# Opening stage of a cross-attention and local-attention kernel: loading, turning, normalising and projecting tokens by groups of four batches

## The reference, cut to what matters

```
z  = (x - mean(x)) / sqrt(var(x) + 1e-5)           # layer norm without scale
Q  = z @ Wq + bq ;  K = ctx @ Wk + bk ;  V = ctx @ Wv + bv
for each batch and head:                           # the "attention steps"
    p = softmax(Q_h @ K_h.T / sqrt(8)) ;  o_h = p @ V_h
x  = x + concat(o_h) @ Wo + bo
# bv is folded into the output: bo + bv @ Wo
```

## Time and profile before

| | |
|---|---|
| median of 3 runs | 2327.3 us (2323.77 to 2329.75) |
| the profiled execution | 2321.82 us, span of the profile 2320.0 us |
| busy: PE, DVE, ACT, POOL | 2133.4, 1756.9, 1709.5, 1339.4 us |
| granted clock of TensorE, mean | 0.981 |

### The profile page before, as it was taken

The page is one execution under the profiler, slowest core; times in us unless marked ns, Lnnn a source line. Parts: engine busy times, 40 slices in busy tenths (PEclk is TensorE's granted clock), DMA queues, the critical chain, the costliest instruction groups (busy, mean ns, idle before and its releaser), DMA issues. The chain is left out here.

```text
span 2320.0 us, 88291 instructions
## 1 busy us (share of the span) xinstructions
PE 2133.4 (92%) x33770; PEld 1456.9 (63%) x33770; DVE 1756.9 (76%) x4926; ACT 1709.5 (74%) x5910; POOL 1339.4 (58%) x1270
## 2 busy tenths in 40 slices
PE   6989999999999999999999999999999877899997
PEld 4656766666666666666666666666666664666663
DVE  3888877778777778777878777878777487888863
ACT  3767878877778787877888677877787544787872
POOL 1337757666666666666666566666666125666650
PEclk8999999999999999999999999999999998999998
DMA  4001221112211212112211122211121100000000
GB/s 110 4 3 34 72 55 47 39 48 66 54 41 43 62 49 55 43 44 62 57 47 41 39 67 57 49 35 47 50 55 41 44 15 6 13 17 11 15 11 23
DMA packets 141519, 96.93 MB, mean 42 GB/s; under 512 B 61832, under 2 KB 133040, under 8 KB 141104
## 3 DMA queue, kind: packets, MB, share of 16 engines
q1 hardware_dynamic: 141104, 91.28, 15.6%
HBM read 23.11 MB, written 1.05 MB: 10 GB/s over the span
## 5 line engine op out<-in xcount | busy, mean ns | idle before, releaser
L715 PE MATMUL bank<-wqkv,hs 128*128 128x512 f32 x1344 | 671.2, 618 | 20.3 <-ACT arena L1438 13.8
L1712 POOL TENSOR_TENSOR arena<-arena,rnorm 128x512 f32<-128x512 f32 x448 | 455.1, 1044 | 385.9 <-DVE rnorm L1963 384.6
L1705 POOL TENSOR_TENSOR arena<-arena 128x512 f32<-128x512 f32 x448 | 567.3, 1273 | 138.3 <-DVE arena L1912 138.1
L1407 ACT ACTIVATE arena<-bank,amx 128x64 f32<-128x64 f32 x1536 | 457.6, 334 | 7.5 <-DVE amx L1978 7.2
L1907 DVE TENSOR_TENSOR arena<-bank,rot 128x512 f32<-128x512 f32 x448 | 306.4, 684 | 88.3 <-PE bank L715 85.2
L1384 ACT ACTIVATE arena<-bank 128x512 f32<-128x512 f32 x448 | 264.1, 616 | 133.8 <-PE bank L736 132.6
L715 PEld LDWEIGHTS bank<-wqkv,hs 128*128 128x128 f32 x1344 | 229.9, 192 | 202.5 <-issue 153.6
L1407 ACT ACTIVATION_READ_ACCUMULATOR arena<-bank,amx 128x1 f32 x1536 | 351.1, 229 | 0.0
L1912 DVE TENSOR_TENSOR arena<-bank,rot 128x256 f32<-128x256 f32 x896 | 332.9, 412 | 0.0
L736 PEld LDWEIGHTS bank<-ident,arena 128*128 128x128 f32 x1792 | 213.3, 143 | 152.2 <-issue 129.1
L1919 DVE TENSOR_REDUCE ss<-arena 128x8 f32<-128x512 f32 x448 | 283.2, 669 | 32.3 <-ACT arena L1378 32.1
(11 more groups left out here) (179 smaller groups left out, 3218.0 us busy)
## 6 DMA issues: line engine op xcount, KB each, us to landing
arena<-arena SPq DMA_DIRECT2D x768, 64.0 KB
wqkv<-in_L_ffn_Wqkv_dram SPq DMA_DIRECT2D x24, 256.0 KB, 3.2
hs<-z SPq DMA_DIRECT2D x128, 32.0 KB, 1.8
fx<-z SPq DMA_DIRECT2D x32, 128.0 KB, 2.2
hs<-z SPq DMA_DIRECT2D x128, 31.8 KB, 1.9
fx<-z SPq DMA_DIRECT2D x32, 127.0 KB, 2.5
wqkv<-in_L_ffn_Wqkv_dram SPq DMA_DIRECT2D x24, 128.0 KB, 2.6
w<-in_L_ffn_W_dram SPq DMA_DIRECT2D x6, 341.0 KB
```

The lines of the kernel that those rows point to most:

```text
L715: nc.tensor.matmul(bank[o][:], src[:], wqkv[w][:, off:off + 512], start=True, stop=True).then_inc(AT[name] if part < 2 else AT[name][i], 1)
L1407: ins = nc.scalar.activation(pb[i][0][p % 2][:, h * DH:(h + 1) * DH], bank[3 + g][:, j * DH:(j + 1) * DH], ACT.Exp, bias=amx[p % 2][:, i, ...
L1705: nc.gpsimd.tensor_tensor(t, t, rs[i][c], ALU.add).then_inc(AT["ak" if c else "aq"][i], 1)
L1712: nc.gpsimd.tensor_tensor(t, t, rnorm[p % 2][:, i, HU * c:HU * c + HU].unsqueeze(2).to_broadcast([P, HU, DH]), ALU.mult).then_inc(AT["mk" ...
```

## The change

- `x` and the context land in four pieces each, by groups of four batches, with a semaphore for each group; the identity is the first load, and the other constants are spread behind the pieces. They land in tiles of their own (`raw_x`, `raw_c`), so `cen` and `dev` are no longer landing places.
- The eight loads of cross-attention weights and biases are issued by ACT on its own DMA queue.
- PE, ACT and DVE get a new order for the opening stage: the work is interleaved by group. The reciprocal square root runs once for group 0 (`pe_var(0, 1)`) and once for groups 1 to 3 (`pe_var(1, 4)`), so its 11 DVE instructions run twice. Attention steps 0 and 1 stand inside this order; group 3 is projected after step 1.
- The bfloat16 identity and the masks are made on ACT between attention steps 1 and 2.
- POOL waits for the keys and values of the group that it needs, not for all.
- Later users of the shared semaphores get other counts; nothing is changed behind attention step 16 but a wait of PE for the masks.

Core of the diff (the functions `tokens`, `context`, `x_keys` and so on are the old operations on one group):

```diff
-            sp.dma_start(cen.rearrange("p (b d) -> p b d", b=NB), A["x"].rearrange("b t d -> t b d")).then_inc(ld_x, 16)
-            sp.dma_start(dev.rearrange("p (b d) -> p b d", b=NB), A["ctx_1024"].rearrange("b t d -> t b d")).then_inc(ld_x, 16)
+            def load_tokens(k):
+                for dst, name in ((raw_x, "x"), (raw_c, "ctx_1024")):
+                    sp.dma_start(quads(group(dst, k)), A[name][4 * k:4 * k + 4].rearrange("b t d -> t b d")).then_inc(ld_x[k], 16)
+            sp.dma_start(ident[:], c_ident).then_inc(ld_x[0], 16)
+            load_tokens(0)
+            load_tokens(1)
+            sp.dma_start(head_m[:], c_head).then_inc(ld_c, 16)
+            load_tokens(2)
+            load_tokens(3)
+            sp.dma_start(v_mask[:], c_vmask.rearrange("p (h d) -> p h d", h=4)).then_inc(ld_c, 16)
...
         @block.tensor
+            turn_tokens(0)
+            turn_tokens(1)
+            pe.wait_ge(c_pool, 1)
+            first_mean(0, 4)
+            pe.wait_ge(ld_xw, 8 * 16)
+            x_keys(0, 5)
+            x_values_in(0, 6)
+            first_mean(1, 7)
+            pe_var(pe, 0, 1, 4)
+            turn_tokens(2)
+            pe.wait_ge(XP["dve"], K_READY[0])
+            x_keys(1, 5)
+            pe.wait_ge(XP["act"], V_READY[0])
+            x_values_in(1, 6)
+            turn_tokens(3)
+            first_broadcast(0, 4)
+            first_mean(2, 0)
+            first_mean(3, 2)
+            pe.wait_ge(in_act, 3)
+            x_queries(0, 1)
+            pe_var(pe, 1, 4, 7)
+            x_step(0)
+            pe.wait_ge(LN["xn"], 1)
+            first_broadcast(1, 4)
+            pe.wait_ge(XP["dve"], K_READY[1])
+            first_broadcast(2, 5)
+            pe.wait_ge(XP["act"], V_READY[1])
+            first_broadcast(3, 6)
+            x_queries(1, 7)
+            pe.wait_ge(LN["xn"], 2)
+            x_keys(2, 4)
+            pe.wait_ge(LN["xn"], 3)
+            x_values_in(2, 5)
+            pe.wait_ge(LN["xn"], 4)
+            x_queries(2, 6)
+            pe.wait_ge(XP["dve"], K_READY[2])
+            pe.wait_ge(XP["act"], V_READY[2])
+            x_step(1)
+            pe.wait_ge(XP["act"], Q_READY[1])
+            x_keys(3, 7)
+            pe.wait_ge(XP["act"], Q_READY[2])
+            x_values_in(3, 6)
+            pe.wait_ge(XP["dve"], K_READY[3])
+            x_queries(3, 7)
+            pe.wait_ge(XP["act"], Q_READY[3])
+            nc.tensor.matmul(bank[7][:, 256:257], xwo[:], xbv[:], start=True, stop=True).then_inc(X0["y"], 1)
+            for s in range(2, NB + 1):
+                x_step(s)
...
         @block.scalar
+            for i, n in enumerate(("Wq", "Wk", "Wv")):
+                act.dma_start(xw[:, i, :], A["L0_xattn_" + n]).then_inc(ld_xw, 16)
+            for i, n in enumerate(("bq", "bk", "bo")):
+                act.dma_start(xb[:, i:i + 1], col(A["L0_xattn_" + n])).then_inc(ld_xw, 16)
+            act.dma_start(xbv[:], col(A["L0_xattn_bv"])).then_inc(ld_xw, 16)
+            act.dma_start(xwo[:], A["L0_xattn_Wo"]).then_inc(ld_xw, 16)
...
+            context(0)
+            act_square(act, 0, 0)
+            x_values_in(0, 2, 6)
+            context(1)
+            act_square(act, 0, 1)
+            context(2)
+            x_values_in(1, 4, 6)
+            context(3)
+            x_queries(0, 5, 1)
+            act_square(act, 0, 2)
+            act_square(act, 0, 3)
+            x_step(0)
+            x_queries(1, 6, 7)
+            x_values_in(2, 8, 5)
+            x_queries(2, 9, 6)
+            x_step(1)
+            x_values_in(3, 11, 6)
+            x_queries(3, 12, 7)
+            masks()
+            for s in range(2, NB + 2):
+                x_step(s)
...
         @block.gpsimd
-            pool.wait_ge(XP["qe"], NBLK)
-            pool.wait_ge(XP["ve"], NBLK)
-            pool.wait_ge(XP["ke"], NBLK)
+                    pool.wait_ge(XP["act"], V_READY[b // 4])
+                    pool.wait_ge(XP["dve"], K_READY[s // 4])
...
         @block.vector
+            tokens(0)
+            tokens(1)
+            dve_centre(dve, 0, 0, 4, base_x)
+            dve.wait_ge(ld_xw, 8 * 16)
+            nc.vector.tensor_scalar(xbq[:], xb[:, 0:1], float(1 / np.sqrt(XD)), None, ALU.mult).then_inc(XP["dve"], 1)
+            x_keys(0, 1, 5)
+            dve_centre(dve, 0, 1, 7, base_x)
+            first_newton(0, 1, 4)
+            tokens(2)
+            x_keys(1, 3, 5)
+            tokens(3)
+            dve_normalise(dve, 0, 0, 4, z)
+            dve_centre(dve, 0, 2, 0, base_x)
+            dve_centre(dve, 0, 3, 2, base_x)
+            first_newton(1, 4, 7)
+            x_step(0)
+            for k in range(1, NBLK):
+                dve_normalise(dve, 0, k, 3 + k, z)
+            x_keys(2, 7, 4)
+            x_step(1)
+            x_keys(3, 10, 7)
```

More of the change, by code:

```diff
@@ L112, in build @@
         arena = sb("arena", [P, 49 * BLK])
-        cen = arena[:, 8 * TOK:9 * TOK]
-        dev = arena[:, 9 * TOK:10 * TOK]
+        raw_x, raw_c, cen, dev = (arena[:, i * TOK:(i + 1) * TOK] for i in range(4))
         slot = lambda i: arena[:, i * BLK:(i + 1) * BLK]
@@ L237, in pe_mean, with pe_var @@
                              ).then_inc(LN["mean"], 1)
[L239 to L244, removed]
+        def pe_var(pe, first, last, o):
+            pe.wait_ge(LN["sq"], last)
+            for b in range(4 * first, 4 * last):
+                c = 2 * (b - 4 * first)
+                mm = nc.tensor.matmul(bank[o][:, c:c + 2], dev[:, b * P:(b + 1) * P], mean_w[:, 0:2], start=True, stop=True)
+            mm.then_inc(LN["var"], 1)
         def pe_broadcast(k, o):
@@ L590, in _, with turn_tokens @@
         def _(pe):
-            pe.wait_ge(ld_x, 32)
-            pe.wait_ge(ld_c, 96)
-            for src, o in ((cen, 0), (dev, 4)):
-                for k in range(NBLK):
+            def turn_tokens(k):
+                pe.wait_ge(ld_x[k], 48 if k == 0 else 32)
+                for src, o in ((raw_x, 0), (raw_c, 1)):
+                    o += 2 * (k % 2)
+                    if k >= 2:
+                        pe.wait_ge(in_act if o % 2 else io_dve, k - 1)
                     for j in range(4):
@@ new lines, in _, with context @@
+            for i, n in enumerate(("Wq", "Wk", "Wv")):
[4 more added lines that the diff above has]
+            act.dma_start(xwo[:], A["L0_xattn_Wo"]).then_inc(ld_xw, 16)
+            def context(k):
+                act.wait_ge(io_ps, 2 * k + 2)
+                nc.scalar.activation(group(ctx_t, k), bank[1 + 2 * (k % 2)][:], ACT.Copy).then_inc(in_act, 1)
@@ new lines, in x_values_in, with x_queries, masks @@
+            def x_values_in(k, n, o):
+                act.wait_ge(XP["p"], n)
+                nc.scalar.activation(group(x_v, k), bank[o][:], ACT.Copy).then_inc(XP["act"], 1)
+            def x_queries(k, n, o):
+                act.wait_ge(XP["p"], n)
+                act.wait_ge(XP["dve"], BQ_READY)
+                nc.scalar.activation(group(x_q, k), bank[o][:], ACT.Identity, bias=xbq[:, 0:1], scale=float(1 / np.sqrt(XD))
+                                     ).then_inc(XP["act"], 1)
+            def masks():
+                act.wait_ge(ld_c, 80)
+                nc.scalar.activation(ident_b[:], ident[:], ACT.Copy).then_inc(XP["act"], 1)
+                for n in range(2):
+                    for a in range(2):
+                        w = DH if n == 0 else P
+                        o = 2 * DH * n + w * a
+                        nc.scalar.activation(mask_b[n][:, a], mask_f[:, o:o + w].unsqueeze(1).to_broadcast([P, 4, w]), ACT.Copy
+                                             ).then_inc(XP["act"], 1)
@@ L2256, in y_gate @@
                 ins.then_inc(YP["gt"], 1)
-            for s in range(NB + 1):
+            tokens(0)
[19 more added lines that the diff above has]
+            x_keys(3, 10, 7)
+            dve.wait_ge(X0["y"], 1)
+            nc.vector.tensor_tensor(xbo[:], bank[7][:, 256:257], xb[:, 2:3], ALU.add).then_inc(XP["dve"], 1)
+            for s in range(2, NB + 1):
                 x_step(s)
```

140 lines of the change are left out of this document (42 added, 98 removed).

## The result

| | us |
|---|---|
| before, median of 5 runs | 2324.69 (2322.69 to 2329.75) |
| after, median of 5 runs | 2311.74 (2302.56 to 2317.28) |
| ratio after / before | 0.9937, 95% interval 0.9915 to 0.9958 |
| profiled execution of after, its span | 2317.28, 2315.5 |

The change gains 13 us by the medians, 14.6 by the ratio (0.63% of 2324.7); I had said 9.6. The opening is almost what was forecast: the scores of batch 3 start at 58.40 us instead of 66.92. The surplus lies behind them, where I had expected nothing.

A forecast was written before the change was run, and what follows sets the result against it. PE was taken as the bound, with gains possible only in the first 66.92 us. Load and regrouping 12.6 us less low clock 3.0 gave 9.6 us, so 2327.3 would become 2317.7 us, range 2311 to 2324.

The forecast's parts named there:

- the low clock: PE in the opening: one fall to 1.2 GHz between 24 and 31 us, costing 3.0 us (2.5 to 6).
- whatever it moves there shifts all that follows by the same amount: Behind the first 66.92 us: only semaphore counts change, so scores 3 to the end stays 2253.1 us, within 2 us.
- Both signs of being wrong: Prediction wrong if the stretch behind scores 3 changes by over 2 us, or PE waits for DMA after 8 us.
- group 1: Opening load: the second four batches' tokens and context land at 7.9 us, bounds 6.8 to 9.5.
- turning 2 begins: PE in the opening: transposes of group 2 start at 13.95 us, without a gap before, four transposes priced 0.78 us.
- idle ahead of squares 1 to 3: PE in the opening: an added wait of 2.4 us from 22.45 us, released by ACT's square.
- The rival of late tokens: Load: pieces and 4-byte bias rows lower the rate, group 1 at 10.4 us; gain 7.1, time 2320.2; chance 0.10.
- First root: DVE in the opening: group 0's square root takes 2.3 us, done at 16.5 us while PE is busy.
- my rival of a double fall: Opening clock: low through steps 0, 1 and group 3, or twice; gain 6.6 or less, 2321 us; chance 0.15.
- Masks: ACT between attention steps 1 and 2: making them delays the values of batch 0 by 1.25 us (0 to 2.06).
- The second queue: Load: ACT's queue adds no bandwidth; weights ahead take 0.9 us of group 0's 6.0 us.
- the slower rival: Attention steps: clock stays at 1.2 GHz, each step costs 2.2 us more, eight steps give 2332 us; chance 0.05.

The follow-up runs named there:

- preheat: Changed kernel with sixteen unread 128x128 products on PE ahead of the first transpose; 2314.69 us in one execution.
- one_queue: Changed kernel with its eight weight and bias loads issued by SP behind the tokens of group 1 instead of by ACT; 2306.03 us, ratio 0.9919.
- bias_late: Changed kernel with the four 4-byte-row bias loads moved from ACT's queue to SP's, behind tokens and context of group 2; 2313.76 us in one execution.
- squares_first: Changed kernel with ACT's squares of groups 2 and 3 put ahead of its copy of queries 0; 2315.17 us in one execution.
- warm: Changed kernel with four unread 128x512 products in PE's gaps, two before the squares, two behind attention step 0; 2315.75 us in one execution.
- masks_early: Changed kernel with ACT making the identity and masks ahead of attention step 0; 2307.24 us in one execution.
- four_edits: Changed kernel with later bias loads, POOL held to the first normalised group, squares ahead of queries 0, and masks ahead of attention step 0; 2303.02 us, ratio 0.9907.
- four_preheat: The same kernel as four_edits plus sixteen unread 128x128 products on PE before the tokens land; 2306.34 us, ratio 0.9917.
- delayed: Changed kernel with ten unread 128x512 products on PE ahead of attention step 2, measured twice; 2310.66 and 2312.86 us.
- pool_late: Changed kernel with POOL's first masked keys and values waiting for the first normalised group; 2316.05 us in one execution.

## Why the prediction was right or wrong

In the opening the mechanism was right, and nearly the size: scores 3 forecast at 57.3 us with the low clock, measured at 58.40 and 57.04. The step that failed is the first: "whatever it moves there shifts all that follows by the same amount", with 2253.1 us behind scores 3 as the test. It agrees with before's order (7 us later, 5 to 7 us more), but between the two orders the rest shrinks by about 7 us, from 2257.6 to 2250.8 in the means of the runs. The opening itself gave 8.4 us, 1.2 less than the 9.6 of the sum; so the surplus behind it is more than the whole difference between 9.6 and the measured 13 to 15. Half of it goes with fewer microseconds of low clock, and its cause stays open. My bound of 2 us on that stretch was too narrow in any case: in single executions of one and the same kernel it moved by 6 us (2253.1 and 2259.7 in two profiles of before).

Both signs of being wrong that I had named came: that stretch changed by more than 2 us, and PE waited for a DMA until 9.36 us. That the median, 2311.74 us, still lies in my range is no merit. The range began at 2311, while the bounds of my own sum end at 14.9 us of gain, which is 2312.4.

Point by point, forecast against the profile of after:

| step | forecast | measured |
|---|---|---|
| group 0 | 6.0 | 6.01 |
| group 1 | 7.9 | 9.36 |
| turning 2 begins | 13.95 | 16.71 |
| queries 0 done | 22.45 | 25.0 |
| idle ahead of squares 1 to 3 | 2.4 | 1.81 |
| scores 0, at full clock | 27.7 | 31.61 |
| scores 1, low clock counted | 40.5 | 41.02 |
| scores 2, low clock counted | 49.8 | 49.76 |
| scores 3, low clock counted | 57.3 | 58.40 |

That scores 1 and 2 agree within 0.6 us is luck. By the end of queries 0 PE is 2.6 us late, by the tokens, by turnings at 1.2 GHz and by the root. The wait ahead of the squares, the steps behind them (18.15 us from scores 0 to scores 2, forecast 19.1) and the low clock (2.4 instead of 3.0) each came out smaller than taken, and made up for it.

- Group 1: late by 1.46 us, inside its bounds (9.5). The rival of late tokens had the right cause, the 4-byte rows; it had asked for 10.4 us. I had put it aside because of the rate of 512-byte rows, which says nothing of pieces of 4 bytes.
- Turning 2: late by another 1.3 us. Half of the opening's first products ran at 1.2 GHz. My price of 0.78 us for four transposes was a mean over both levels; the profiles of after and preheat give 0.98 and 0.52. Because the high error stands in the first turnings and the low one in the later, it partly cancelled.
- First root: taken as 2.3 us in cover, it was 4.3 us and out of cover by 0.8, since POOL's masked keys now fall into it. I had said of them only that they lie far ahead of 27.65 us; when a step moves ahead, what it then runs beside has to be checked too.
- Squares: the wait is there, the releaser as named, 1.8 instead of 2.4 us; from the order of ACT alone 1.2 of it can be had back.
- Low clock: one fall forecast for 24 to 31 us, worth 3.0. It came at 26.6 us, cost about 2 us in the squares (4.82 us, against 2.85 in the second profile of after, where the clock was still high) and 0.4 in the queries of group 1. The second, at 51 us, cost 1.5 and was no part of the sum; my rival of a double fall had foreseen it, at 3 us instead of 1.5.
- Masks: the wait 1.25 us forecast, 0.93 measured, and the low stretch behind it.
- The second queue brings no bandwidth: in one_queue group 0 lands 0.9 us sooner without the weights beside it, as their bytes over the rate had said.
- The attention steps stayed at full clock from 58 us on; the slower rival had no case.

## What to carry to other kernels

Work that can begin early belongs into the gaps of a preparation that runs through several engines: here two attention steps among the projections gave 6.5 us, some 2.6 of it escaped low clock, and the finer loading and projecting alone 1.9, hardly clear of the spread. When a piece moves, list what it now runs beside: the same edit brought POOL onto DVE's root, 4-byte loads onto the tokens and the masks out of their cover, and four small edits against these and ACT's order gave 7 to 8 us more. A forecast of a difference should take unit prices at one clock level, and treat an untouched stretch of 2250 us as known to no better than the executions of one kernel agree.

## What the runs showed of the hardware beyond that

- TensorE starts a kernel at 1.2 GHz, though the profile's clock column says 1.00 there: 8 transposes 1.97 us at the start, 1.04 behind 16 other products, and in before 10 and then 19 transposes in 2 us.
- A POOL operation on 128x512 holds up DVE operations of 0.16 us that read SBUF too until it ends (0.96 and 1.20 us); the one that reads PSUM beside it took 0.16.
- Four loads of 128 pieces of 4 bytes beside the tokens took the rate of 16 DMA engines from about 280 to 172 GB/s for two microseconds (bias_late against after), with the engines' share down to 0.42.
- A fall of the clock followed the wait of 0.93 us behind the masks in six profiles (both of after, one_queue, squares_first, warm, preheat), and there is none at that place in the five without the wait (masks_early, four_edits, four_preheat, both of delayed); but in bias_late and pool_late the wait stood and the clock stayed. A wait of that size makes the fall possible, not certain.
